# A decoder kernel: the state-space scan in four passes of two channel chunks, its decay and state in PSUM

## The reference

```python
A = -jnp.exp(A_log)
dt = jax.nn.softplus(dbc[..., :1] * dt_w + dt_b)
Bp = dbc[..., 1:1 + D_STATE]
Cp = dbc[..., 1 + D_STATE:]
def step(h, inp):
    x_t, dt_t, B_t, C_t = inp
    A_bar = jnp.exp(dt_t[..., None] * A)
    h = A_bar * h + dt_t[..., None] * B_t[:, None, :] * x_t[..., None]
    y_t = jnp.einsum('bdn,bn->bd', h, C_t)
    return (h, y_t)
...
y = jnp.moveaxis(ys, 0, 1) + xc * D
y = y * jax.nn.silu(z)
return y @ W_out + residual
```

## Time and profile before

| what | value |
|---|---|
| median of three runs | 2721.99 us (2719.16 to 2728.14) |
| span of the profiled execution, first to last instruction | 2718.7 us |
| DVE busy in it | 1901.3 us, 70% |
| PE busy | 2083.7 us, 77% |
| POOL busy | 955.0 us, 35% |
| ACT busy | 979.9 us, 36% |
| first scan to the last product with the gate | about 157 to 781 us of the span |
| mean granted clock of TensorE, of full speed | 0.870 |

### The profile page before, as it was taken

One profiled execution on the slowest core, in us unless ns is written; L12 is line 12 of the kernel. 1 busy time (PEld: TensorE's weight loads), 2 busy tenths in 40 slices (PEclk: granted clock), 3 DMA queues, 4 the chain that ended last, 5 costly groups with the idle time before them and its releaser, 6 DMA issues. The chain is left out here.

```text
span 2718.7 us, 36741 instructions
## 1 busy us (share of the span) xinstructions
PE 2083.7 (77%) x10486; PEld 1140.3 (42%) x10486; DVE 1901.3 (70%) x3096; ACT 979.9 (36%) x1976; POOL 955.0 (35%) x603
## 2 busy tenths in 40 slices
PE   6945555655576888887779999997888779994777
PEld 2311212212233666653333333335544436561677
DVE  5679999999956777766755555555643356667894
ACT  2732222222203777762355555551122111111221
POOL 1056665666614222200036666661000002231232
PEclk8967776777787999998979999998999789996788
DMA  1011111111105665533015554535201151116320
GB/s 57 0 52 46 48 46 54 41 41 54 53 8 135 151 137 131 138 75 113 1 53 177 169 169 145 161 105 171 94 0 34 22 162 70 62 62 206 120 77 27
DMA packets 128350, 235.59 MB, mean 87 GB/s; under 512 B 33606, under 2 KB 88807, under 8 KB 125720
## 3 DMA queue, kind: packets, MB, share of 16 engines
q1 hardware_dynamic: 110648, 191.60, 24.2%
q0 software_dynamic: 13824, 37.77, 4.4%
q10 hardware_dynamic: 3808, 5.38, 0.7%
HBM read 185.25 MB, written 49.44 MB: 86 GB/s over the span
## 5 line engine op out<-in xcount | busy, mean ns | idle before, releaser
L551 PE MATMUL mamba_y<-mamba_read,ident 128*128 128x448 f32 x512 | 331.7, 797 | 272.0 <-DVE mamba_read L521 272.0
L492 POOL TENSOR_TENSOR xn<-mamba_u,mamba_b_all 128x896 f32<-128x896 f32 x128 | 395.3, 3113 | 328.8 <-DMA mamba_b_all<-mamba_b 251.4
L514 DVE TENSOR_TENSOR_SCAN mamba_state<-mamba_decay,xn 128x896 f32<-128x896 f32 x128 | 378.1, 2963 | 5.2 <-ACT mamba_decay L481 5.2
L551 PEld LDWEIGHTS mamba_y<-mamba_read,ident 128*128 128x128 f32 x512 | 124.6, 266 | 478.9 <-DVE mamba_read L521 397.6
L481 ACT ACTIVATE mamba_decay<-mamba_dt,mamba_small 128x888 f32<-128x888 f32 x128 | 132.2, 1035 | 439.5 <-DVE mamba_state L514 439.4
L521 DVE TENSOR_TENSOR mamba_read<-mamba_state,mamba_c_all 128x896 f32<-128x896 f32 x128 | 249.4, 1958 | 0.0
L2377 ACT ACTIVATE moe_w_tile<-moe_w 128x1216 f32 x144 | 175.1, 1217 | 145.1 <-PE moe_y_ps L2329 130.1
L2314 PE MATMUL moe_up_ps<-moe_w_tile,moe_xT 128*64 128x352 f32 x1152 | 204.3, 476 | 1.4 <-issue 1.3
L962 DVE CUSTOM_DVE_ANT_0 xattn_sm<-xattn_s_ps,xattn_mask 112x375 f32<-112x375 f32 x256 | 138.6, 545 | 82.8 <-PE xattn_s_ps L855 71.7
L2276 POOL DMA_INDIRECT moe_y<-moe_y_sb,moe_index x144 | 155.9, 1082 | 112.6 <-DVE moe_y_sb L2350 86.9
L1053 ACT ACTIVATE xattn_prob<-xattn_sm,xattn_least 112x375 f32<-112x375 f32 x256 | 154.4, 604 | 74.3 <-DVE xattn_least L962 70.1
(11 more groups left out here) (309 smaller groups left out, 3819.8 us busy)
## 6 DMA issues: line engine op xcount, KB each, us to landing
moe_w<-moe_w SPq DMA_DIRECT2D x64, 480.0 KB
soft_w<-soft_w SPq DMA_DIRECT2D x16, 1024.0 KB, 8.5
mamba_b_all<-mamba_b SPq DMA_DIRECT2D x32, 448.0 KB, 3.5
mamba_c_all<-mamba_c SPq DMA_DIRECT2D x32, 448.0 KB, 4.6
moe_f_part<-moe_y SPq DMA_DIRECT2D x14, 1024.0 KB, 5.6
soft_logits<-soft_logit SPq DMA_DIRECT2D x28, 512.0 KB, 2.6
soft_logit<-soft_logits SPq DMA_DIRECT2D x14, 1024.0 KB, 5.1
xattn_ks<-xattn_k_parts SPq DMA_DIRECT2D x32, 375.0 KB, 6.7
```

The source lines that it names most:

```text
L492: pool.tensor_tensor(fed[:, c], u[:, c, tok], b_all[:, s], ALU.mult).then_inc(input_ready, 1)
L514: dve.tensor_tensor_scan(state[:, q % DIC], decay[:, q % DIC], fed[:, q % DIC], 0.0, ALU.mult, ALU.add).then_inc(state_ready, 1)
L551: mm = pe.matmul(y[:, q % DIC, w, 0:CW], g.ident[:], read[:, q % 2, w * CW:(w + 1) * CW], start=False, stop=False, skip_group_check=True)
```

## The change

The four chunks are taken two at a time (`PAIR` = 2), so that the two halves become four passes: chunks 0 and 1 with the first half of the tokens and then the second, and chunks 2 and 3 likewise. A pass has 32 units (`UNITS`), and the body of a loop holds four. `y` needs four banks then, and the other four hold `state`, two slots of two banks. ACT writes the decay straight into a slot; the scan reads it there and writes the state over it, element by element; the product with C reads the slot. ACT waits for the product two units before (`out_ready`), since a slot is free only then. The scan no longer waits for `out_ready`. As the slot's first places of each sequence are overwritten, ACT writes them each time, as exp(-3e38), which is zero (line 487 of the changed kernel). DVE issues the product directly behind its own scan. B and C are loaded twice, once for each pair of chunks: 64 rows each in place of 32. `fed` still has four buffers, and the products with the gate are four after each pass.

```diff
-            QH = NST * DIC
+            PAIR, RING = 2, 4
+            UNITS = NST * PAIR
+            passes = [(c0, hh) for c0 in range(0, DIC, PAIR) for hh in range(2)]
...
-                decay = k.sb(c2, "mamba_decay", [P, DIC, HW])
-                state = k.sb(c2, "mamba_state", [P, DIC, HW])
+                never = k.sb(c2, "mamba_never", [P, BPH, 1])
...
-                y = k.ps(c2, "mamba_y", [P, DIC, 2, 512])
+                y = k.ps(c2, "mamba_y", [P, PAIR, 2, 512])
+                state = k.ps(c2, "mamba_state", [P, 2, 1024])
...
+                by_batch = [state[:, s, 0:HW].rearrange("p (b l) -> p b l", l=L) for s in range(2)]
...
+                    for again in range(2):
+                        before = 2 * NST * again
+                        with loop(sp, 2 * NST - 2, 2) as n:
+                            for s in range(2):
+
+                                sp.wait_ge(out_ready, 2 + PAIR * (before + n + s + 1))
+                                after_wait(sp, g)
+                                load(sp, n + s + 2, s)
+                        if again == 0:
+                            for s in range(2):
+                                sp.wait_ge(out_ready, 2 + PAIR * (2 * NST - 2 + s + 1))
+                                load(sp, s, s)
...
-                                    act.wait_ge(state_ready, hh * QH + DIC * (n + s) + c + 1)
-                                    src = dt[:, c, tok].rearrange("p (b l) -> p b l", l=L)
-
-                                    act.activation(by_batch[c][:, :, 1:], src[:, :, 1:], ACT.Exp, scale=a_neg[:, c, ds(n + s, 1)]).then_inc(decay_ready, 1)
+                                    act.wait_ge(out_ready, p * UNITS + PAIR * (n + s) + c + 1)
+                                    act.activation(by_batch[c][:, :, 0:1], never[:], ACT.Exp)
+                                    src = dt[:, c0 + c, tok].rearrange("p (b l) -> p b l", l=L)
+                                    act.activation(by_batch[c][:, :, 1:], src[:, :, 1:], ACT.Exp, scale=a_neg[:, c0 + c, ds(n + s, 1)]).then_inc(decay_ready, 1)
...
-                                pool.wait_ge(b_loaded[s], 8 * NST * hh + 8 * n + 16)
-                                for c in range(DIC):
-                                    pool.wait_ge(state_ready, hh * QH + DIC * (n + s) + c + 1)
-                                    pool.tensor_tensor(fed[:, c], u[:, c, tok], b_all[:, s], ALU.mult).then_inc(input_ready, 1)
+                                pool.wait_ge(b_loaded[s], 8 * NST * p + 8 * n + 16)
+                                for c in range(PAIR):
+                                    pool.wait_ge(state_ready, p * UNITS + PAIR * (n + s) + c + 1)
+                                    pool.tensor_tensor(fed[:, PAIR * s + c], u[:, c0 + c, tok], b_all[:, s], ALU.mult).then_inc(input_ready, 1)
...
-                    for c in range(DIC):
-                        zeros = dve.memset(by_batch[c][:, :, 0:1], 0.0)
-                    zeros.then_inc(state_ready, DIC)
+                    dve.memset(never[:], -BIG).then_inc(state_ready, RING)
...
-                                dve.wait_ge(out_ready, q0 + q)
-                                dve.tensor_tensor_scan(state[:, q % DIC], decay[:, q % DIC], fed[:, q % DIC], 0.0, ALU.mult, ALU.add).then_inc(state_ready, 1)
+                                dve.tensor_tensor_scan(state[:, q % 2, 0:HW], state[:, q % 2, 0:HW], fed[:, q % RING], 0.0, ALU.mult, ALU.add).then_inc(state_ready, 1)
...
-                                dve.wait_ge(state_ready, q0 + q + DIC + 1)
+                                dve.wait_ge(state_ready, q0 + q + RING + 1)
                                 dve.wait_ge(summed, q0 + q + 1)
-                                dve.tensor_tensor(read[:, q % 2], state[:, q % DIC], c_all[:, q // DIC], ALU.mult).then_inc(out_ready, 1)
-
-                            scan(0)
-                            for q in range(1, 2 * DIC):
+                                dve.tensor_tensor(read[:, q % 2], state[:, q % 2, 0:HW], c_all[:, q // PAIR], ALU.mult).then_inc(out_ready, 1)
+
+                            for q in range(2 * PAIR):
                                 scan(q)
-                                read_out(q - 1)
-                            read_out(2 * DIC - 1)
-                        dve.wait_ge(y_ready, hh + 1)
+                                read_out(q)
+                        dve.wait_ge(y_ready, p + 1)
```

More of the change, by code:

```diff
@@ L444, in mamba, with load @@
                 c_all = k.sb(c2, "mamba_c_all", [P, 2, HW])
-                decay = k.sb(c2, "mamba_decay", [P, DIC, HW])
                 fed = g.xn[:].rearrange("p h (s t) -> p (h s) t", t=HW)
-                state = k.sb(c2, "mamba_state", [P, DIC, HW])
+                never = k.sb(c2, "mamba_never", [P, BPH, 1])
                 read = k.sb(c2, "mamba_read", [P, 2, HW])
                 skip_diag = k.sb(c2, "mamba_skip_diag", [P, DIC, P])
-                y = k.ps(c2, "mamba_y", [P, DIC, 2, 512])
+                y = k.ps(c2, "mamba_y", [P, PAIR, 2, 512])
+                state = k.ps(c2, "mamba_state", [P, 2, 1024])
                 block = c2.enter_context(nc.Block())
-                by_batch = [decay[:, c].rearrange("p (b l) -> p b l", l=L) for c in range(DIC)]
-                def load(sp, n, s):
-                    sp.dma_start(b_all[:, s], b_dram[ds(n, 1), :].partition_broadcast(P)).then_inc(b_loaded[s], 16)
-                    sp.dma_start(c_all[:, s], c_dram[ds(n, 1), :].partition_broadcast(P)).then_inc(c_loaded[s], 16)
+                by_batch = [state[:, s, 0:HW].rearrange("p (b l) -> p b l", l=L) for s in range(2)]
+                def load(sp, row, s):
+                    sp.dma_start(b_all[:, s], b_dram[ds(row, 1), :].partition_broadcast(P)).then_inc(b_loaded[s], 16)
+                    sp.dma_start(c_all[:, s], c_dram[ds(row, 1), :].partition_broadcast(P)).then_inc(c_loaded[s], 16)
                 @block.sync
@@ L461, in _ @@
                         load(sp, s, s)
-                    with loop(sp, 2 * NST - 2, 2) as n:
-                        for s in range(2):
-                            sp.wait_ge(out_ready, 2 + DIC * (n + s + 1))
-                            after_wait(sp, g)
-                            load(sp, n + s + 2, s)
+                    for again in range(2):
[9 more added lines that the diff above has]
+                                load(sp, s, s)
                 @block.scalar
                 def _(act):
-                    for hh in range(2):
+                    act.wait_ge(state_ready, RING)
+                    for p, (c0, hh) in enumerate(passes):
                         tok = slice(hh * HW, (hh + 1) * HW)
@@ L498, in _ @@
                     diag.then_inc(skip_ready, 1)
-                    for c in range(DIC):
-                        zeros = dve.memset(by_batch[c][:, :, 0:1], 0.0)
-                    zeros.then_inc(state_ready, DIC)
+                    dve.memset(never[:], -BIG).then_inc(state_ready, RING)
                     dve.memset(read[:, :, 0:1], 0.0).then_inc(out_ready, 2)
-                    for hh in range(2):
-                        tok = slice(hh * HW, (hh + 1) * HW)
+                    for p, (c0, hh) in enumerate(passes):
                         with loop(dve, NST, 2) as n:
-                            q0 = hh * QH + DIC * n
+                            q0 = p * UNITS + PAIR * n
                             def scan(q):
@@ L536, in _ @@
                     pe.wait_ge(skip_ready, 1)
-                    for hh in range(2):
-                        if hh:
-                            pe.wait_ge(y_done, 2 * DIC * hh)
-                        for c in range(DIC):
+                    for p, (c0, hh) in enumerate(passes):
+                        if p:
+                            pe.wait_ge(y_done, 2 * PAIR * p)
+                        for c in range(PAIR):
                             for w in range(2):
                                 part = slice(hh * HW + w * CW, hh * HW + (w + 1) * CW)
-                                mm = pe.matmul(y[:, c, w, 0:CW], skip_diag[:, c], xs[:, c, part], start=True, stop=False, skip_group_check=True)
-                        if hh == 0:
+                                mm = pe.matmul(y[:, c, w, 0:CW], skip_diag[:, c0 + c], xs[:, c0 + c, part], start=True, stop=False, skip_group_check=True)
+                        if p == 0:
                             mm.then_inc(summed, 2)
                         with loop(pe, NST, 2) as n:
-                            for q in range(2 * DIC):
-                                pe.wait_ge(out_ready, hh * QH + DIC * n + q + 3)
+                            for q in range(2 * PAIR):
+                                pe.wait_ge(out_ready, p * UNITS + PAIR * n + q + 3)
                                 for w in range(2):
-                                    mm = pe.matmul(y[:, q % DIC, w, 0:CW], g.ident[:], read[:, q % 2, w * CW:(w + 1) * CW], start=False, stop=False, skip_group_check=True)
```

(1 more changed line is left out.)

11 lines of the change are left out of this document (6 added, 5 removed).

## The result

| | before | changed |
|---|---|---|
| median of four runs each | 2725.06 us (2719.16 to 2729.11) | 2510.01 us (2509.35 to 2515.33) |
| ratio | | 0.9214, 95% interval 0.9197 to 0.9231 |
| span of the profiled execution | 2718.7 us | 2507.6 us |
| first scan to the last product with the gate ("the stretch" below) | 624.2 us | 412.1 us |
| rest of the span | 2094.5 us | 2095.5 us |

The account below looks back on a forecast made before the run. DVE, held up by POOL, was taken to bound the two passes. 236.8 - 7.7 - 12.8 - 2 - 5.4 = 208.9 us less gave 2513 us, range 2498 to 2535, or 2496 to 2592 with late rows and PE.

Parts of the forecast that it names:

- collision gone: In the two passes, scans and products with one operand in PSUM no longer stand still beside POOL: 236.8 us less.
- product directly behind its scan: On DVE, each product waits for the scan just ahead and comes 0.10 us later: 12.8 us more.
- PSUM for scan and product: On DVE, a PSUM operand costs 0.03 us for each scan and product: 7.7 us more for 128 units.
- late rows of B: Loads of B's rows, needed every two units: 2 us more taken for the scatter of their landings.
- two more seams: Between passes, four seams totalling 19.1 us in place of 13.7: 5.4 us more.
- the slow scan: Rival: the scan in place in PSUM reads and writes one bank by turns, 128 us more, 2641 us; chance 0.08.
- the rival on the slower side: Rival: the collision stays since fed and C remain in SBUF, 2748 us; chance 0.07, including a scan equally slow.
- The chain of B: From freed slot through B's landing and POOL to the scan: 6.1 us a state against DVE's 6.16, hidden by 0.06.
- The rival of late rows: Rows of B land late: 2541 us at landings of 4.5 us, 2589 at worst; chance 0.12.
- The rival of the lower clock: PE stays at the lower clock, 3.36 + 0.05 us a unit in place of 3.08: 42 us, 2555 us; chance 0.04.
- The signs named beforehand: Changed profile: scan 2.0 to 2.1 us, product near 1.09, POOL about 2.1, product 0.03 after scan, passes 98.6, seams 4.8.

Follow-up runs that it names:

- light kernels in SBUF: The kernel before with POOL multiplying 8 of 896 columns: 2634.33 us; the same with each product issued directly behind its scan: 2651.09 us.
- half exchanged: The changed kernel with only the decay in PSUM, state in SBUF: 2712.28 us; with only the state in PSUM, decay in SBUF: 2787.5 us.

## Why the prediction was right, step by step

| term | forecast us | measured us | by |
|---|---|---|---|
| collision gone | -236.8 | -234.5 | POOL with 8 columns, before |
| product directly behind its scan | +12.8 | +18.8 | unit 2.92 to 3.067 in the two light kernels in SBUF, x 128 |
| PSUM for scan and product | +7.7 | 0 | 2020 against 2021 and 1090 against 1092 ns |
| late rows of B | +2 | +2.0 | 412.1 - 410.1, 24 late scans |
| two more seams | +5.4 | +3.0 | 4 x 4.17 against 6.8 + 6.9 |
| sum | -208.9 | -210.7 (stretch: -212.1) | |

**The collision.** The step that a hindered scan stands still and then does its whole work, and that it ends with one operand in PSUM, held; 1.4 us of the stretch's 212.1 are left over by the terms, about what two readings of one stretch differ by. The earlier trace rows were a product and a subtraction, not a scan; that the scan, and a DVE write into PSUM, would behave so was a guess from them, and the spread of 2020 to 2032 ns bears it out. With it fall the slow scan and the rival on the slower side. The Trainium skill (SBUF — State Buffer, section on the two separate sides) says that a DVE instruction with two SBUF inputs and a GpSimd instruction that reads SBUF exclude each other for a whole instruction: the timelines of the kernels with slots in SBUF and with the half exchanged agree, down to the scan that writes SBUF and is free (2.01 us).

**PSUM's price and the order's.** These two terms were mis-sized, in opposite ways: 7.7 + 12.8 = 20.5 forecast, 18.8 measured, all of it the order's. That they nearly cancel is luck, and the unit's 3.07 us against the forecast's 3.08 is no proof of either. The 30 ns between the earlier trace rows came from comparing a product that waits for nothing recent with a subtraction that had waited; it is not PSUM's. Of the order's 0.147 us for a unit, 0.11 lie between scan and product (0.04 of gap in place of 0.07 of overlap) and the rest in the durations (10 and 30 ns more). The stretches of the two light kernels in SBUF differ by more, 20.5 us: the first products of the one with the direct order wait 3.3 us longer for PE (3.7 + 1.6 against 1.5 + 0.5), and its seams are shorter. The errata's 65 ns for a source in PSUM, weighed in the forecast, show nowhere at this size, and that a semaphore costs nothing extra, as in eight copies, does not carry over to a product directly behind its scan (both in the Trainium skill, VectorE: DVE Perf Modes, sections on the TRN2 errata and on the DRAIN).

**The chain of B.** Worked out at 0.06 us of room, read at 0.07, and its loss at half of each delay confirmed by the kernel that delays it: 1.6 us later would give 64 x (0.8 - 0.07) = 47 us, and 44 were measured. The rival of late rows had its mechanism right and its condition absent: landings stayed at 3.5 us in the median beside twice the rows (141 and 145 GB/s in the windows, where it was 43 and 45). The 2 us for the scatter were a guess, and came out.

**The seams.** 4.17 us each in place of 4.8: the wait for PE's last matmuls was 1.98 us and not 2.6. This is in the main the new order, as the seams of the two light kernels in SBUF show, at a granted clock of 1.00 in both:

```profile
349.62 4.34 DVE L532 TENSOR_TENSOR mamba_xs<-mamba_y,mamba_gate 128x448 f32<-128x448 f32 x8 [2.48 <-PE mamba_y L553]
...
357.84 4.34 DVE L530 TENSOR_TENSOR mamba_xs<-mamba_y,mamba_gate 128x448 f32<-128x448 f32 x8 [1.98 <-PE mamba_y L551]
```

In the first, and in the kernel before, the last two products of a half stand back to back, and PE still has the matmuls of both to do; directly behind their scans they lie a scan apart, and only the last one's are left. That is 0.50 us. The lower clock of the earlier trace rows (0.75 in the wait of 2.64 us) is the other 0.16. The forecast priced the new order at the products and overlooked what it gives back at the seams.

**PE.** It costs nothing: outside the seams DVE never waits for it. The rival of the lower clock did not come: 1.00 was granted from 165 to 460 us, 295 us at a stretch, with a unit's matmuls at 1.77 of 3.07 us. Before, they took 3.36 us of 4.77 where it was at the lower level.

```profile
165.00:460.00 295.00, 172.25 (x394) 66.36 (x393) 287.35 (x195) 112.55 (x193) 189.40 (x93) 1.00 0.45 146
```

The window's columns are those of the earlier trace rows; 1.00 is 2.4 GHz. **ACT** was early everywhere: from the end of the product (299.14 + 1.09 = 300.23) to the decay's (300.38 + 1.00 = 301.38) are 1.15 us where the forecast had 1.5.

The signs named beforehand came, but for the length of the seams: scan 2.0 to 2.1 in median and maximum, product 1.09, POOL 2.08, product 0.04 after its scan, passes of 98.7, 98.4, 99.0 and 99.4 us. No DVE wait for ACT.

## What to carry to other kernels

Where VectorE and GpSimd each read two operands from SBUF, look for an unhindered instruction in the timeline. The mean of its group less its duration, times the count, is what moving a single operand to PSUM can bring (here for scan and product together 237 us), and both kinds of hindered instructions have to be moved for it. Then add the price of the new order between dependent instructions, about 0.15 us each here, and follow the chain of the transfer that now comes twice as often: room of 0.06 us held, and 1.6 us of delay cost 44. Once the collision is gone, the other engine is worth work of its own.

## What was not expected of the hardware

- The engine that hinders is hindered too, by about as much an instruction: POOL's multiplication took 3113 ns before, 2078 alone, and in the half exchanged kernels 2475 and 3005. The loss depends on which instructions meet: with the scan free, 63 of 128 products still met POOL.
- A scan of 896 elements costs 2.01 to 2.02 us whether it reads and writes SBUF, reads PSUM and writes SBUF (2012 ns), or reads and overwrites the same PSUM bank (2020 ns). ACT is 35 ns faster into PSUM than into SBUF at 888 elements (1000 against 1035).
- An instruction that waits for the one ahead of it on DVE shows up longer by itself: the product 1092 in place of 1062 ns, the scan behind it 2021 in place of 2011.
- Left open: where a multiplication falls. It starts at a landing, and no run sets that place on purpose, so the 53 and 121 us of the two half exchanged kernels are read and not forecast.
